# Second scan stage: the copy of a chunk's sums at the first place of the next chunk, and all side work one unit earlier

## The reference, cut to what matters

```python
delta = jax.nn.softplus(x @ W_delta + b_delta)
Bm, Cm = x @ W_B, x @ W_C
A = -jnp.exp(A_log)                       # D=256 channels, S=16 states
def step(h, inp):
    x_t, d_t, B_t, C_t = inp
    bar_A = jnp.exp(jnp.minimum(d_t[..., None] * A, 10.0))
    bar_B = jnp.clip(d_t[..., None] * B_t[:, None, :], -10.0, 10.0)
    h = jnp.clip(bar_A * h + bar_B * x_t[..., None], -10000.0, 10000.0)
    y_t = jnp.sum(h * C_t[:, None, :], axis=-1) + x_t * D_param
    return (h, y_t)
```

## Time and profile before

| | |
|---|---|
| time, median of 3 runs | 4958.69 us (4956.91 to 4969.4) |
| the profiled execution: its time, its span | 4959.75 us, 4958.0 us |
| mean granted TensorE clock | 0.88 |
| busy share of the span: PE, DVE, ACT, POOL | 79%, 57%, 45%, 50% |
| this stage's eight chunks, from VectorE's first scan to its last product | 2382.9 to 2890.6 us of the span |

### The profile page before, as it was taken

The page is one execution under the profiler, slowest core; times in us unless marked ns, Lnnn a source line. Parts: engine busy times, 40 slices in busy tenths (PEclk is TensorE's granted clock), DMA queues, the critical chain, the costliest instruction groups (busy, mean ns, idle before and its releaser), DMA issues.

```text
span 4958.0 us, 49367 instructions
## 1 busy us (share of the span) xinstructions
PE 3917.7 (79%) x15216; PEld 2269.9 (46%) x15218; DVE 2847.6 (57%) x4916; ACT 2214.3 (45%) x4082; POOL 2468.8 (50%) x2152
## 2 busy tenths in 40 slices
PE   6888888759957888797677869994884698888892
PEld 2333333347734556576333336663572233334571
DVE  5999999951136665211688862226433676764522
ACT  5565656421136775111555533333243455555241
POOL 5999999922212234211789854442355422222256
PEclk8999999959978889898788879995996699998896
DMA  5556556522210010321455531115155422221145
GB/s 152 157 162 159 157 157 163 145 77 85 83 54 17 18 35 26 102 87 62 132 159 145 145 106 45 45 42 159 36 160 121 127 41 40 43 37 55 39 141 132
DMA packets 312121, 476.73 MB, mean 96 GB/s; under 512 B 34890, under 2 KB 167990, under 8 KB 311786
## 3 DMA queue, kind: packets, MB, share of 16 engines
q1 hardware_dynamic: 277152, 388.87, 28.6%
q0 software_dynamic: 29184, 76.12, 5.5%
q10 hardware_dynamic: 5504, 8.39, 0.6%
HBM read 375.26 MB, written 97.49 MB: 95 GB/s over the span
## 4 chain that ended last, share of the span: by engine, by line
PE 37%; POOL 6%; DVE 5%; issue 4%; DMA 4%; ACT 3%; SPq 0%; DVEq 0%; ACTq 0%; POOLq 0%
PE s_gate_up L2325 8%; PE s_result_sum L2341 4%; PE s_hidden_sum L1761 3%; PE s_result_sum L1772 3%; PE s_out_sum L3696 3%; POOL s_h L435 2%; PE s_shared L2981 2%; PE s_scores L3637 2%; DVE s_maxima L3328 2%; PE s_scores_T L3680 2%; PE s_shared L2991 1%; POOL s_gathered L1047 1%; POOL s_h L444 1%; PE s_transposed L2315 1%; PE s_mid_transposed L2334 1%
## 5 line engine op out<-in xcount | busy, mean ns | idle before, releaser
L435 POOL TENSOR_TENSOR s_h<-s_dtu,s_bc 128x1024 f32<-128x1024 f32 x384 | 902.3, 2357 | 71.7 <-PE s_y_sum L477 56.1
L477 PE MATMUL s_y_sum<-s_h,identity 128*128 128x512 f32 x1536 | 776.6, 644 | 145.6 <-POOL s_h L444 132.1
L402 ACT ACTIVATE s_decay<-s_dt,s_A 128x512 f32<-128x512 f32 x768 | 498.5, 682 | 333.3 <-DVE s_h L377 326.5
L477 PEld LDWEIGHTS s_y_sum<-s_h,identity 128*128 128x128 f32 x1536 | 296.8, 203 | 586.9 <-issue 312.5
L2325 PE MATMUL s_gate_up<-s_w_gate_up,s_rowsT 128*128 x1184 | 420.2, 487 | 2.1 <-issue 1.9
L3502 ACT ACTIVATE s_weights_T<-s_scores_T 128x1024 f32<-128x1024 f32 (+3 forms) x384 | 292.6, 811 | 256.4 <-PE s_scores_T L3680 254.8
L3328 DVE TENSOR_REDUCE s_maxima<-s_scores 128x1 f32<-128x512 f32 (+3 forms) x463 | 296.7, 659 | 178.2 <-PE s_scores L3641 96.7
L444 POOL TENSOR_TENSOR s_h<-s_h,s_bc 128x512 f32<-128x512 f32 x288 | 365.8, 1271 | 27.8 <-DVE s_h L370 19.4
L2384 DVE TENSOR_TENSOR s_mid<-s_act,s_gate_up 128x128 f32<-128x128 f32 (+1 forms) x228 | 92.8, 407 | 451.0 <-ACT s_act L2357 451.0
L3550 POOL TENSOR_SCALAR_AFFINE_SELECT s_weights_T<-s_weights_T 128x256 f32<-128x256 f32 x256 | 102.7, 406 | 468.6 <-ACT s_weights_T L3502 465.9
L370 DVE TENSOR_TENSOR_SCAN s_decay<-s_decay,s_carry,s_h 128x512 f32<-128x512 f32 x240 | 305.4, 1288 | 24.8 <-POOL s_clip_flag L2653 11.2
(11 more groups left out here) (533 smaller groups left out, 7690.6 us busy)
## 6 DMA issues: line engine op xcount, KB each, us to landing
s_bc<-s_bc_rows SPq DMA_DIRECT2D x384, 512.0 KB, 5.2
sorted_results<-s_result SPq DMA_DIRECT2D x160, 128.0 KB, 2.2
s_w_inter<-in_L_ffn_experts_inter SPq DMA_DIRECT2D x16, 1024.0 KB, 5.0
s_w_exp_out<-in_L_ffn_experts_out SPq DMA_DIRECT2D x16, 1024.0 KB, 8.3
s_queries<-parts_of_q SPq DMA_DIRECT2D x96, 128.0 KB, 4.6
s_keys<-parts_of_k SPq DMA_DIRECT2D x96, 128.0 KB, 7.5
results_by_token<-zeros SPq DMA_DIRECT2D x16, 512.0 KB, 5.8
s_pair<-results_by_token SPq DMA_DIRECT2D x16, 512.0 KB
```

The source lines that it names most:

```text
L402: S.e.activation(self.decay[:, (2 * g + d) % 4, :], dt[q // self.passes % 2][:, at, :], ACT.Exp, scale=A[:, at, g % ns:g % ns + 1]).then_i ...
L435: G.e.tensor_tensor(self.h[r][:], dtu[q // self.passes % 2][:, at:at + 2, :], mid(self.bc[r][:, 0, :], 2), ALU.mult).then_inc(*self.fed.up())
L477: made = T.e.matmul(self.y[:, d, :], ident[:], self.h[r][:, d, :], start=False, stop=g % ns == ns - 1)
```

## The change

All side work of the stage is yielded two ticks, one unit, sooner, on all engines. Two pieces on ScalarE are moved otherwise: the copy of the sums from tick 3 to tick 0, and the pair weights from tick 0 to tick 1, so that the copy now stands ahead of them and directly behind decays(16c+2). No instruction is added, removed or resized.

```diff
 def vector():        # VectorE
     def early(c):
-            yield 10
+            yield 8
...
-            yield 11
+            yield 9
             V.wait_ge(*added.at(c))
-            yield from ln.vector_stats(c, x4, 11)
+            yield from ln.vector_stats(c, x4, 9)
     def front(c):
-            yield 18
+            yield 16
...
-            yield 24
+            yield 22
...
-            yield 25
+            yield 23
...
-            yield 28
+            yield 26
...
-            yield 30
+            yield 28
...
 def scalar():        # ScalarE
     def early(c):
-            yield 0
+            yield 1
             pairs.scalar_weights(c)
-            yield 18
+            yield 16
...
-                yield 19 + t
+                yield 17 + t
     def front(c):
-            yield 13
+            yield 11
...
-            yield 15
+            yield 13
...
-            yield 20
+            yield 18
...
-            yield 27
+            yield 25
     def back(c):
-            yield 3
+            yield 0
             S.wait_ge(*sc.summed.at((c + 1) * NS - 1))
             S.wait_ge(*logit_made.at(c - 1))
             S.e.activation(y[:], sc.y[:], ACT.Copy).then_inc(*sc.y_taken.up())
-            yield 27
+            yield 25
...
-            yield 30
+            yield 28
...
 def gpsimd():        # GpSimd
     def early(c):
-            yield 16
+            yield 14
     def front(c):
-            yield 25
+            yield 23
...
-            yield 31
+            yield 29
...
 def tensor():        # TensorE
     def early(c):
-            yield 6
+            yield 4
     def front(c):
-            yield 11
+            yield 9
...
-            yield 14
+            yield 12
...
-            yield 17
+            yield 15
...
-            yield 29
+            yield 27
     def back(c):
-            yield 25
+            yield 23
...
-            yield 29
+            yield 27
```

## The result

The changed kernel takes 4933.1 us (median of 4 runs, 4923.57 to 4934.19) against 4959.36 us (4956.91 to 4969.4) of the kernel before in the same session: a ratio of 0.9939 with a 95% interval of 0.9927 to 0.9952. Between the medians that is a gain of 26.3 us, by the ratio some 30 (24 to 36). The forecast was 4934 us. The profiled execution took 4932.84 us with a span of 4931.1 us, 26.9 us shorter than the span before.

A forecast was written before the change was run, and what follows sets the result against it. No engine was full: the stage lost at most about 70 us in VectorE's idle time, where side work and recurrence meet. Per-chunk idle savings summed to 25.1 us off 4959.75 us, giving 4934 us, range 4921 to 4950.

The forecast's parts named there:

- The copy and L472: After the chunk's first scan: copy at 4.5 us, L472 from 5.5 to 9.2, seventh feed about 14.6, eighth 17.0.
- rival (d): ScalarE stands at tick 0 waiting for the last total, delaying decays(3) and VectorE; slower, 4974 us, chance 0.04.
- rival (c): L472 at the higher clock (1.9 us off GpSimd's wait), flag's reading hidden; 9 us more gain, 4925 us, chance 0.17.
- Rival (b): GpSimd sets the pace, with the pair sum at the lower clock, up to 4.87 us; 4947 us, chance 0.17.
- The pair sum: VectorE's wait at L2494, 13.9 us over five chunks, goes; gain 2.8 us a chunk.
- The loss ahead of the fourth unit: Copy and weights ahead of decays(3) delay VectorE's fourth-unit scan: 1.0 us lost in even chunks, 0.6 in odd.
- Softplus: VectorE asks one product sooner after ScalarE starts softplus: 0.6 us lost, its wait becomes 1.8 us a chunk.
- The sums of |dtu|: VectorE's wait for ScalarE's sums keeps its order one unit sooner: unchanged at 2.9 us a chunk, 20.4 in seven.
- L2518: VectorE's wait for three small matmuls, put in at about 0.3 us a chunk.
- The flag: GpSimd's flag comes 3.6 us sooner in its queue; idle at a chunk's first scan shrinks to 0.6 us, bounds 0 and 1.3.
- The sum: Gains of all chunks from idle time before less after: 25.1 us in the stage, giving 4934 us.
- The two rules: Skill's rules on GpSimd's SBUF contention, which rows were said to speak against, and TensorE's clock; the sum used L472's slow value.

The follow-up runs named there:

- second execution: The changed kernel run once more with no edit, beside two later kernels; ratio 0.9941 to the kernel before, stage 475.24 us.
- late flag: The changed kernel with only GpSimd's clip flag put back from tick 29 to tick 31; ratio 0.9965 to the kernel before, stage 494.94 us.
- shift alone: The changed kernel with the copy back at tick 3 and pair weights at tick 0; ratio 0.9956 to the kernel before, stage 493.73 us.

## Why the prediction was right, step by step

**The copy and L472.** Copy at V+4.5, L472 at V+5.5: measured V+4.4 and V+5.4. An idle ScalarE at tick 0, the slower rival (d), occurred at one boundary of seven and for 0.47 us; at the others the copy follows decays(2) directly. The time of L472 was a mis-sized term: "What TensorE does behind a gap of some 4 us no row of mine shows; the sum goes by the slow value". In six boundaries of seven it ran in 1.98 us, in the other in 2.63. So the seventh feed ran at V+12.9 without a wait, not at V+14.6, and the eighth at V+15.2, not V+17.0. That half of rival (c) came true, and the wait for the seventh feed, which was to stay, went too. It gave VectorE nothing that shows, as no wait of VectorE for a feed is in this trace to be shortened: GpSimd used the lead to reach a wait for the sums in the middle of the chunk (3.46 us at 2549.92), since TensorE stands 3.85 us for `s_xT` in its own queue and has its delta matmuls ahead of the totals. Rival (b), GpSimd as the bound with a pair sum at the lower clock, did not occur either: in chunks 1 to 5 L1104 took 3.62 us four times and 3.86 once.

**The pair sum.** Forecast 13.9 us of wait gone: gone. The kernel with the copy alone and the one with `early` unmoved show that the copy's place did this. The argument had given it jointly to the copy and to tick 4, and that division was wrong: the gain at L2494 needs no shift.

**The loss ahead of the fourth unit.** Forecast 1.0 us more in even chunks, to 1.3, and 0.6 in odd ones. Measured idle time there: 1.27 and 0.95 in the even chunks 2 and 4, and 0.81, 0.25 and 0.25 in the odd ones, so right to high.

**Softplus.** Forecast 1.8 us a chunk, measured 1.62 to 2.01 in six and 3.53 in chunk 6, which was 2.00 in the second execution. The term is right but for that one chunk, which gained 1.1 us and not 2.2. TensorE shows why, first in the execution of the result, then in the second:

```profile
2777.31 3.62 PE L2683 MATMUL s_front<-s_xT,s_w_bc 128*32 128x512 f32 x4 [3.83 <-ACT s_xT L2583]
```

```profile
2769.38 1.90 PE L2683 MATMUL s_front<-s_xT,s_w_bc 128*32 128x512 f32 x4 [2.46 <-ACT s_xT L2583]
```

Behind 3.83 us without work these matmuls ran at a granted clock of 0.50, the lower level (1.2 GHz); the totals and the delta matmuls behind them ended later (33.1 us after the chunk's first scan, 30.6 in the second execution), and ScalarE waited 1.44 us for these ahead of softplus. In the second execution TensorE had stood 2.46 us, the clock was 1.00 (2.4 GHz), and ScalarE did not wait. The kernel with the weights at tick 2 repeats the first case: 3.89 us, 3.62 us, a wait of ScalarE of 1.56 us and 3.65 us at L2508. So TensorE's wait for `s_xT`, which the forecast put at nothing, costs some 1.5 us in chunk 6.

**The sums of |dtu|.** Forecast unchanged at 2.9: 20.4 us in seven, unchanged. **L2518.** 0.3 us a chunk were put in for the three small matmuls; no wait is in the trace. Chunks 3 to 5 gained 15.1 us where 4.6 + 4.2 + 2.7 = 11.5 were expected; of these 3.6, L2518 makes 0.9, the fourth unit (0.6 + 1.3 + 0.6 forecast, 1.45 measured) 1.05, the three first scans behind them (1.8 forecast, 0.1 + 0.46 + 0 measured) 1.2, and the pair sum of chunk 4 (0.3 forecast, none measured) 0.3.

**The flag.** Forecast 0.6 us at each first scan, from bounds of 0 and 1.3. Measured 1.86, 0, 1.45, 0.1, 0.46, 0 and 0.62, a sum of 4.5 where 0.6 x 7 = 4.2 were put in. The mean was good, in part by luck (2.8 in the second execution), and single values follow from when the flag comes. In chunk 2 the scan starts 1.3 us behind the flag's end (2573.19 to 2574.51) and VectorE's last product ends 0.14 ahead of the flag: the 1.45 us are the reading in full, the upper bound. Where the flag comes while products run, the reading is hidden and the idle time 0. The 1.86 us stand at the end of chunk 0, where GpSimd is the fullest (59.53 busy of 64.96) and the flag, at 2450.13, is itself 0.9 us late. The experiment with the late flag shows the step: with it 17 of the stage's 28 us are lost.

**The sum.** Forecast per chunk 3.2, 3.7, 4.5, 4.6, 4.2, 2.7, 2.2, 0; measured 3.3, 4.7, 4.0, 5.9, 5.1, 4.2, 1.1, 0.1. The 28.4 us of the stage became 26.9 of the span and 26.3 between the medians. The forecast was 3.3 us short for the stage, and the spread between two executions (2.8 us) is nearly as large. That the time came out within 1 us of 4934 is in part luck: in the profiled execution the 3.3 us were taken back by a stage that happened to start 3.2 us later.

**The two rules.** By the Trainium skill, GPSIMD Engine Reference, section Specifications, GpSimd contends with VectorE's instructions of two SBUF inputs. The prediction took its rows as evidence against a stretching of the feeds by this rule; that reading was wrong, since they don't test it. VectorE's scans and products take the decays from PSUM, its two additions (L2494, L2508) take `s_front` from PSUM, and read only one other tensor, from SBUF. L435 takes 2.35 us in chunk 7, where VectorE is busy all of 49.67 us, as everywhere else; with two inputs from SBUF no run here shows it. The other, from TensorE: Matmul & The Clock Gate, "Part 1: The HAM clock gate", that TensorE loses its rate by idling and keeps it under work, had the right direction, and the measured 1.98 us, at a granted clock of 1.00 in the stretch of chunk 2, sides with it against the value that the sum used.

## What to carry to other kernels

Where an engine reads a flag that another computes, look at what stands ahead of the flag in that engine's queue: here one product and one feed (3.6 us) ahead of six tiny instructions cost 17 us over seven boundaries, and giving GpSimd time earlier in the chunk, by the copy alone, took nothing off the idle time there (22.9 us for 22.2). Asking later for a result helps only if the engine that makes it isn't also the next to be needed: at the softplus most of the wait changed its name from `s_dt` to decays, and taking work out of ScalarE's long piece made it 1.0 us shorter in each of six chunks. In a schedule of ticks, test each half of a change alone and read single chunks: two movements of 3.5 us cancelled in one of these kernels.

## What the runs showed of the hardware

**TensorE's clock behind short gaps.** L472 is the same four matmuls behind a gap in seven boundaries of every kernel. TensorE's timeline in the kernel with the copy alone and in the changed one:

```profile
2454.70 3.78 PE L472 MATMUL s_y_sum<-s_xT,s_skip_diagonals 128*128 128x512 f32 x4 [7.24 <-ACT s_y L2609]
...
2517.43 3.09 PE L472 MATMUL s_y_sum<-s_xT,s_skip_diagonals 128*128 128x512 f32 x4 [3.02 <-ACT s_y L2609]
```

```profile
2457.03 1.98 PE L472 MATMUL s_y_sum<-s_xT,s_skip_diagonals 128*128 128x512 f32 x4 [1.11 <-ACT s_y L2609]
...
2579.88 2.63 PE L472 MATMUL s_y_sum<-s_xT,s_skip_diagonals 128*128 128x512 f32 x4 [2.58 <-ACT s_y L2609]
2640.94 1.98 PE L472 MATMUL s_y_sum<-s_xT,s_skip_diagonals 128*128 128x512 f32 x4 [3.27 <-ACT s_y L2609]
```

Behind gaps of 4.08 us and more it took 3.14 to 3.78 us in every boundary of three kernels (copy alone, shift alone, late flag). In the changed kernel, behind 1.11 to 3.27 us, it took 1.98 in six of seven. The granted clock is 0.52 in the stretch of L472 in the earlier trace rows and 1.00 in the changed kernel's 2517.90 to 2519.80, so nearly all at the lower of the two levels (1.2 GHz) and all at the higher (2.4 GHz). It is 0.73 in the 2.63 us at 2579.88, where the level changed on the way. The gap alone doesn't settle it: 3.27 us went with 1.98 in the changed kernel, 2.91 to 3.31 with 3.09 to 3.66 in the one with the copy alone, in the repeated run of the changed kernel 1.92 went with 3.68, and in the one with the weights at tick 2 1.93 with 3.64. Neither half of the change alone reached the higher level regularly (copy alone 3.09 to 3.78, shift alone 3.14 to 3.78); both together did. The early copy is not enough: with the late flag TensorE stands 4.70 to 7.21 us again, although the copy is at tick 0, and L472 takes 3.54 to 3.78. The copy stands behind decays(2), and these wait for VectorE, which waits for the flag.

**Table loads.** Softplus costs ScalarE two loads of 1.28 us a chunk, one ahead of its last pass and one behind it, ahead of decays: 2.6 us of its absence beside 3.1 us of the passes themselves.
